# A decoder layer with a state-space mixer: VectorE takes TensorE's share of the state sum in half of the pairs, and the last attention passes use 512-wide exponentials

## The chip, the cores and the metric

The kernel runs on one core of one Trainium2 chip. The metric is the device time of one execution in microseconds (us). A core has TensorE (PE in the profile, with its weight loads as PEld), VectorE (DVE), ScalarE (ACT), GpSimd (POOL) and SyncE (SP), which here issues every DMA. The engines run their own queues in order and meet only at semaphores.

## The reference

All in fp32, on x of shape 4 x 1024 x 512. The line that matters for the change is the sum over 16 states:

```python
u_act = silu(causal_conv(rmsnorm(x) @ in_proj) + b)        # 1024 channels
dt    = softplus(dt_r @ dt_proj.T + b);  A = -exp(A_log)
h_t   = exp(dt_t * A) * h_(t-1) + dt_t * B_t * u_act_t     # per channel, 16 states
y     = sum over n of h[n] * C[n]  +  D * u_act            # the sum
y     = (y * silu(z)) @ out_proj
h     = x + y;  attn = h + (silu(xn@w1) * (xn@w2)) @ w3    # xn = rmsnorm(h)
x     = layernorm(x + attn)
# cross-attention to 64 keys, 16 heads
p     = softmax(QK/sqrt(32));  t = exp(clip(mlp(mean, max, var of p)))   # one t per batch and head
x     = layernorm(x + softmax(QK / (2 t)) V @ Wo)
# a linear layer with top-2 of 8 low-rank experts
x     = layernorm(x + x @ W.T + b + lora(x))
```

The temperature t needs the first softmax over all 1024 positions of a batch.

## The kernel before

**Chunks.** The 4096 positions are cut into 8 chunks (c = 0 to 7) of 512; two chunks make a batch, so t of a batch is known only after both its chunks, and the second attention pass of chunks 6 and 7 can start only when all else is done.

**Streams.** The work is written as six streams of units: `m` (the mixer: convolution, scan, output projection), `l` (the z gate and dt), `y` (SwiGLU MLP, layernorm, queries), `s` (first attention pass: units sc1, mx, e1, sq, ent), and `x` with `w` (second pass: sc2, e2, flip, val, on, fl2, wo, then the expert layer). A planner, `schedule()`, runs at build time: `m_parts()` and `parts()` give each unit's engine, cost in us and predecessors; it merges the streams into one fixed order for each engine, by when a part could start and by a key from `PHASE`, `WORK` and `LOOK`. It also deals out PSUM banks 4 to 7. So every constant in it can move any unit of any stream. `loads()` orders SP's DMAs by the planned times.

**The scan.** Each chunk has 4 pairs of 128-channel blocks, with 16 states each, so 64 steps. A step k of pair p = k // 16 works on a [128, 2, 512] tile of `hb`, a ring of four:

- POOL, `times_b` (L1017): hb = dtu * B, 1024 wide. It waits until the ring's slot, step k - 4, has been summed (`summed`).
- ACT, `decays` (L1081): two 512-wide exponentials to PSUM banks 0 and 1.
- DVE (L1373): two 512-wide scans. Their length differs a little with the chunk's half.
- POOL, `times_c` (L1027): hb = hb * C, 1024 wide.
- the sum, in PSUM banks 2 and 3 (one for each block of the pair). In chunk 0 PE adds both with an identity product (L1679). In chunks 1 to 7 DVE adds the first block (L1389, 512 wide) and PE the second (L1679). PE starts its bank with a product with the diagonal of D (L1675), DVE's bank is started by an ACT copy of u times D (L1161).

After 16 steps `gate` (L1395) reads both banks. An fp32 product is two matmul records in the trace, so the 576 sums and 36 of the diagonal products of the code show up twice each.

**Between two scans** stand the output projection `out` (L1624), `ht` (L1410 and L1057), the turns, the convolution and dt of the next chunk; POOL's part begins again with du (L1042).

**The attention passes.** In the first, for each 128 positions and each half of the heads (8 heads x 64 keys = 512), DVE takes the maxima (L1462), ACT takes 8 exponentials of 64 with their own bias and accumulated sum (L1252), squares all (L1256), and DVE reduces the squares (L1468). In the second, ACT takes 8 exponentials of 64 with the head's scale and bias and an accumulated sum (L1288); then PE turns them (L1739), multiplies with V (L1747), DVE divides (L1512, L1515), PE turns again (L1753), and `wo` (L1577) and `woa` (L1520) follow.

Of the kernel before, what the change touches and what calls it, by code (L numbers as in the profile page):

```python
# [29 lines left out]
FG = 4  # L30
PE, ACT_, DVE, POOL = "PE", "ACT", "DVE", "POOL"
MM, EV, TURN, HOP, FETCH = 0.87, 0.7, 0.95, 0.2, 5.0
# [16 lines left out]
def dve_first(c, k):  # L49

    return c == 0 and k % 2 == 1 and k > 2

# [54 lines left out]
def s_plan():  # L107
    got = []
    for c in range(CHUNKS):
        for t in range(TT):  # L110
            for hf in range(2):
                got += [("sc1", c, t, hf), ("mx", c, t, hf)] + [("e1", c, t, hf, q) for q in range(3)] + [("sq", c, t, hf)]
# [10 lines left out]
def x_plan(chunks):  # L123
    got = []
    for c in chunks:
        def e2(t, hf):
            return [("e2", c, t, hf, 0), ("e2", c, t, hf, 1)]
# [16 lines left out]
def m_parts(u):  # L144
# [13 lines left out]
    elif kind == "turn_in":  # L158
        part(ACT_, 1.6, ("norm", c))
# [4 lines left out]
    elif kind == "conv":  # L164
        if i < JB:
            part(PE, 4 * MM, ("turn_in", c), ("raw", c, i - 4), name=("up", c, i))
# [13 lines left out]
    elif kind == "rms":  # L180
        part(ACT_, 1.6, *(("ht", c, n) for n in c4s))
        part(DVE, 0.2, mine(0))
        part(ACT_, 1.6, mine(1))
    elif kind == "turn_out":
        for n in c4s:
            part(PE, TURN, ("rms", c))
        for n in c4s:
            part(ACT_, EV, mine(n), ("query", c - 1, KC - 1))
# [9 lines left out]
    elif kind == "step":  # L198
# [8 lines left out]
        if i % NS == 0:  # L207
            part(ACT_, 1.1 if c else 0.5, ("gate", c, i // NS - 1), name=("yp", c, i // NS))
# [14 lines left out]
def parts(u):  # L223
# [27 lines left out]
    elif kind == "sp1":  # L251
        part(ACT_, 3.0, ("dt", *key))
    elif kind == "sp2":
        part(DVE, EV, ("sp1", *key))
    elif kind == "sp3":
        part(ACT_, 2.6, ("sp2", *key))
    elif kind == "sp4":
        part(DVE, 1.6, ("sp3", *key), gives=(("dt", *key),) if i > 1 else ())
# [35 lines left out]
    elif kind == "mx":  # L294
        part(DVE, EV, ("sc1", *key))
    elif kind == "e1":
        part(ACT_, 2.4 if u[4] < 2 else EV, ("mx", *u[1:4]), ("ent", c - 1))
    elif kind == "sq":
        part(DVE, EV, ("e1", *key, 2), gives=(("sc1", *key),))
# [11 lines left out]
    elif kind == "temper":  # L311
        part(DVE, 2.3, ("clip", c), ("e2", c - 2, last, 1, 1), gives=(("mlp", c),))
    elif kind == "sc2":
        part(PE, TURN, ("temper", 2 * b + 1), takes=(u,))
    elif kind == "e2":
        part(ACT_, 2.5, ("sc2", *u[1:4]), ("flip", c, i - 1, u[3]) if i else ("lora", c - 1) if c < CHUNKS - 1 else ("flip", c - 1, last, u[3]), ("val", c, i - 2) if i > 1 else ("val", c - 1, TT - 2 + i),
             gives=(("sc2", *u[1:4]),) if u[4] else ())
    elif kind == "flip":
        part(PE, 0.65, ("e2", *key, 1), takes=(u,))
        part(ACT_, EV, mine(), ("val", c, i - 1) if i else ("val", c - 1, last), gives=(u,))  # L320
    elif kind == "val":
        part(PE, 1.7, ("flip", c, i, 0), ("flip", c, i, 1), takes=(u,))
    elif kind == "on":
        part(DVE, 1.0, ("val", *key), ("fl2", c, i - 1) if i else ("fl2", c - 1, last), gives=(("val", *key),))
# [32 lines left out]
PHASE = {'w': (8.408, 8.256, 8.408, 8.256, 8.639, 8.487, 8.639, 8.487), 'y': (6.039, 6.01, 6.125, 6.218, 6.046, 6.01, 6.051, 6.214), 's': (7.437, 6.89, 7.688, 6.881, 7.587, 6.627, 6.484, 6.736), 'x': (8.713, 8.394, 8.925, 8.582, 8.439, 8.453, 9.268, 6.582)}  # L357
# [153 lines left out]
LOOK = {'w': 0.05, 'm': 0.265, 'l': 0.167, 'x': 0, 'y': 0.277, 's': 0.3}  # L511
# [108 lines left out]
def decoder_layer(nc, A, out):  # L620
# [5 lines left out]
    with ctx:  # L626
# [120 lines left out]
        ln_rstd ln_done xl_var xl_sd xl_rstd xl_done sq_ready mx_ready ent_done kb_sum sta_ready tm_pe tm_act tm_dve tempered e2_ready den_ready  # L747
# [21 lines left out]
        def filled(eng, key):  # L769
# [3 lines left out]
            return ps[:, bank]  # L773

# [1095 lines left out]
```

## Time and profile before

| | |
|---|---|
| time, median of 3 runs | 4144.4 us (4144.25 to 4150.9) |
| the profiled execution | 4142.83 us, span 4141.1 us |
| PE busy | 3648.7 us, 88% |
| DVE, ACT, POOL busy | 2527.0 (61%), 2173.9 (52%), 2481.8 (60%) |
| granted TensorE clock, mean | 0.940 |

The span is that of the first to the last instruction. Busy is the union of an engine's instructions. The output projection of chunk c (L1624) starts at 783.18, 1202.09, 1686.54, 2151.99, 2642.29, 3113.04 and 3581.00 us for c = 1 to 7, and near 368 us for chunk 0. From one such start to the next lie the turn to the next chunk and its scan; this stretch is called the period of chunk c + 1. After 3581 us there is no scan left: that is the tail, of 560 us.

### The profile page before, as it was taken

The numbers are of one execution on the slowest core, as the hardware profiler recorded it, in microseconds if no ns is written. First come the engines' busy times: TensorE is split into PE (matmuls) and PEld (weight loads), VectorE is DVE, ScalarE is ACT, GpSimd is POOL, SyncE is SP. The second block draws the span as 40 slices with busy tenths as digits, with TensorE's granted clock in tenths as the row PEclk, the third lists the DMA queues.
The fourth block names the chain that finished last, engine by engine and source line by source line (L and its number), as shares of the span: only waits on it lengthen the run. The fifth ranks groups of instructions, "written<-read, shape, count | busy, mean of one in ns | idle before, by whom it ended". The sixth has DMA issues, their size and how long they took to land.

```text
span 4141.1 us, 35899 instructions
## 1 busy us (share of the span) xinstructions
PE 3648.7 (88%) x9728; PEld 1712.2 (41%) x9728; DVE 2527.0 (61%) x3294; ACT 2173.9 (52%) x5187; POOL 2481.8 (60%) x1101
## 2 busy tenths in 40 slices
PE   7667998799879998999988998999979998999577
PEld 3223443344334445544434335544334434454243
DVE  4784687567746786267765786367774777422222
ACT  5543544664555556565455456574556457431563
POOL 3885599659964995239972996337991997400000
PEclk9889999999999999999989999999989999999788
DMA  5433354335433442234432453234432443212000
GB/s 176 131 123 103 120 165 152 109 116 165 149 111 113 156 156 81 87 105 154 166 117 97 146 162 110 72 115 144 154 125 84 155 153 116 83 58 87 15 1 21
DMA packets 220834, 481.32 MB, mean 116 GB/s; under 512 B 31836, under 2 KB 32220, under 8 KB 220380
## 3 DMA queue, kind: packets, MB, share of 16 engines
q1 hardware_dynamic: 220636, 479.04, 35.1%
q8 instruction: 81, 1.33, 0.1%
q14 instruction: 117, 0.96, 0.1%
HBM read 468.98 MB, written 9.96 MB: 116 GB/s over the span
## 4 chain that ended last, share of the span: by engine, by line
PE 56%; POOL 7%; ACT 7%; DVE 6%; issue 5%; POOLq 0%; DVEq 0%; ACTq 0%
PE ps L1577 31%; PE ps L1664 7%; PE ps L1679 6%; POOL hb L1027 5%; PE ps L1624 5%; DVE hb L1373 2%; POOL hb L1017 2%; PE ps L1712 1%; ACT xw L1288 1%; PE ps L1747 1%; ACT ps L1252 1%; PE ps L1617 1%; PE ps L1793 1%; PE ps L1780 1%; PE ps L1594 1%
## 5 line engine op out<-in xcount | busy, mean ns | idle before, releaser
L1027 POOL TENSOR_TENSOR hb<-hb,bc 128x1024 f32<-128x1024 f32 x512 | 1227.9, 2401 | 127.6 <-issue 86.9
L1017 POOL TENSOR_TENSOR hb<-dtu,bc 128x1024 f32<-128x1024 f32 x481 | 1134.2, 2359 | 192.3 <-PE ps L1679 128.7
L1081 ACT ACTIVATE ps<-dt,a_neg 128x512 f32<-128x512 f32 x1024 | 697.1, 690 | 853.0 <-DVE hb L1373 848.1
L1577 PE MATMUL ps<-fT,wden 128*128 128x512 f32 x2304 | 1042.7, 601 | 16.1 <-DVE hm L1426 6.7
L1679 PE MATMUL ps<-hb,ident 128*128 128x512 f32 x1152 | 656.7, 672 | 249.5 <-POOL hb L1027 248.2
L1577 PEld LDWEIGHTS ps<-fT,wden 128*128 128x128 f32 x2304 | 442.0, 193 | 577.5 <-issue 573.4
L1373 DVE TENSOR_TENSOR_SCAN hb<-ps,state,hb 128x512 f32<-128x512 f32 x512 | 626.5, 1266 | 42.9 <-ACT ps L1081 28.2
L1373 DVE TENSOR_TENSOR_SCAN hb<-ps,hb 128x512 f32<-128x512 f32 x512 | 593.6, 1204 | 12.5 <-POOL hb L1017 9.0
L1389 DVE TENSOR_TENSOR ps<-ps,hb 128x512 f32<-128x512 f32 x448 | 310.9, 694 | 282.7 <-POOL hb L1027 281.8
L1664 PE MATMUL ps<-wden,hm 128*128 128x512 f32 x1024 | 470.5, 606 | 2.1 <-DVE res L1436 1.9
L1577 PE MATMUL ps<-xnT,wmix 128*128 128x512 f32 x1024 | 456.7, 596 | 13.6 <-ACT xnT L1105 8.2
L1679 PEld LDWEIGHTS ps<-hb,ident 128*128 128x128 f32 x1152 | 220.7, 207 | 590.4 <-POOL hb L1027 402.3
L1042 POOL TENSOR_TENSOR dtu<-dt,u 128x1024 f32<-128x1024 f32 x32 | 75.4, 2356 | 536.8 <-issue 466.8
L1664 PEld LDWEIGHTS ps<-wden,hm 128*128 128x128 f32 x1024 | 198.7, 195 | 260.2 <-issue 246.8
L1577 PEld LDWEIGHTS ps<-xnT,wmix 128*128 128x128 f32 x1024 | 193.9, 191 | 253.6 <-issue 253.3
L1624 PE MATMUL ps<-wmix,u 128*128 128x512 f32 x512 | 221.4, 593 | 6.1 <-DVE u L1395 6.1
L1057 POOL TENSOR_TENSOR res<-bc,res 128x512 f32<-128x512 f32 x32 | 39.5, 1269 | 289.6 <-DVE bc L1410 289.6
L1288 ACT ACTIVATE xw<-ps,nm,ftv 128x64 f32<-128x64 f32 x512 | 199.3, 421 | 17.0 <-PE ps L1712 16.7
L1053 POOL TENSOR_TENSOR res<-res,bo_b 128x512 f32<-128x512 f32 x32 | 39.5, 1270 | 241.8 <-PE ps L1691 241.8
L1203 ACT ACTIVATE hm<-ps 128x512 f32<-128x512 f32 x128 | 75.1, 588 | 201.6 <-PE ps L1577 131.1
L1340 DVE SCALAR_TENSOR_TENSOR hb<-hb,cols 128x512 f32<-128x512 f32 x192 | 143.9, 750 | 37.9 <-ACT hb L1124 33.3
L1436 DVE TENSOR_TENSOR res<-ps,res 128x512 f32<-128x512 f32 x128 | 86.4, 678 | 116.2 <-PE ps L1664 115.4
(207 smaller groups left out, 3995.7 us busy)
## 6 DMA issues: line engine op xcount, KB each, us to landing
bc<-bc_dram SPq DMA_DIRECT2D x1024, 256.0 KB, 3.6
wden<-in_w SPq DMA_DIRECT2D x192, 512.0 KB, 3.6
wmix<-in_w_mix SPq DMA_DIRECT2D x96, 512.0 KB, 3.6
watt<-in_w_qof SPq DMA_DIRECT2D x26, 512.0 KB, 4.3
xm<-in_x SPq DMA_DIRECT2D x8, 1024.0 KB, 5.4
res<-in_x SPq DMA_DIRECT2D x8, 1024.0 KB, 6.8
wden<-in_w_qof SPq DMA_DIRECT2D x16, 512.0 KB, 3.5
out<-res SPq DMA_DIRECT2D x8, 1024.0 KB, 4.3
```

Of the source, the lines that this page charges most:

```text
L1017: TTn(hb[:, k % 4], dtu[:, :, :], bc[:, 0, k % 3].unsqueeze(1).broadcast_to([P, 2, CH]), ALU.mult).then_inc(s.s1_ready, 1)
L1027: TTn(hb[:, k % 4], hb[:, k % 4], bc[:, 1, k % 3].unsqueeze(1).broadcast_to([P, 2, CH]), ALU.mult).then_inc(s.s3_done, 1)
L1081: A_(dst, dt[:, p % 2, jj], ACT.Exp, scale=a_neg[:, j, n:n + 1]).then_inc(full_of(key), 1)
L1288: ins = A_(eb[:, hh], bank[:, h], ACT.Exp, bias=nm2[:, TT * half + i, hh:hh + 1], scale=ftv[:, 0, hh:hh + 1], accum_out=den[:, 0, i % 2, h ...
L1340: ins = V.scalar_tensor_tensor(acc[:, j % 3], up[:, j % 2, tap:tap + CH], conv_w[:, j, tap:tap + 1], acc[:, j % 3], ALU.mult, ALU.add)
L1373: V.tensor_tensor_scan(hb[:, i % 4, jj], src, hb[:, i % 4, jj], first, ALU.mult, ALU.add).then_inc(free_of(key), 1)
L1389: V.tensor_tensor(ps[:, 2], ps[:, 2], hb[:, i % 4, 0], ALU.add).then_inc(s.sum_done, 1)
L1436: V.tensor_tensor(res[:, c % 3, tt], src, res[:, c % 3, tt], ALU.add).then_inc(free_of(key), 1)
L1577: ins = M(dst, a, b, start=start and n == 0, stop=stop and n == len(pairs) - 1)
L1624: ins = M(dst[t], u[:, j, t * P:(t + 1) * P], wo, start=j == 0, stop=j == JB - 1)
L1664: ins = M(dst, hm[:, f, tt * P:(tt + 1) * P], wi[:, (f % 2) * 512:(f % 2) * 512 + 512], start=f == 0, stop=f == FG - 1)
L1679: ins = M(dst, ident[:, :], hb[:, i % 4, jj], start=False, stop=n == NS - 1)
```

## The change

1. **The sum.** `dve_sums(c, p)` is true for c > 0 and p in (0, 3). There DVE adds both blocks in one 1024-wide `tensor_tensor` on banks 2 and 3, PE's products for the pair are dropped, and ACT starts both banks with copies of u times D. Those who wait for a sum there (`summed`: POOL, gate) wait for DVE alone. Pairs 1 and 2 and chunk 0 stay.
2. **First pass of chunk 7** (`wide1`): DVE subtracts the maxima from the scores in PSUM (512 wide), ACT takes one exponential of 512 into `hm`, one square, and DVE reduces both (the sums of the exponentials were accumulated by ACT before).
3. **Second pass of chunks 6 and 7** (`wide2`): `temper` also scales the keys by the head's temperature, PE computes the scores after that, DVE shifts them (new unit `sh`, 512 wide), ACT takes one exponential of 512, DVE reduces it (new unit `dn`), and `on` waits for that.
4. **The planner.** Most costs are set anew (a product 0.87 to 0.866, an eviction 0.7 to 0.61, the first pass's exponentials 2.4 to 1.35, the second's 2.5 to 1.54), with some predecessors, `PHASE` and `LOOK`. All orders are planned again.

```diff
-MM, EV, TURN, HOP, FETCH = 0.87, 0.7, 0.95, 0.2, 5.0
+MM, EV, TURN, HOP, FETCH = 0.866, 0.61, 0.96, 0.19, 5.0
+def dve_sums(c, p):
+    return c and p in (0, 3)
+def pe_pairs(c, p):
+    return len([n for n in range(c * PAIRS + p) if not dve_sums(*divmod(n, PAIRS))])
+def wide1(c):
+    return c == CHUNKS - 1
+def wide2(c):
+    return c >= CHUNKS - 2
...
-LOOK = {'w': 0.05, 'm': 0.265, 'l': 0.167, 'x': 0, 'y': 0.277, 's': 0.3}
+LOOK = {'w': 0.08, 'm': 0.247, 'l': 0.167, 'x': 0, 'y': 0.259, 's': 0.355}
...
+            if dve_sums(c, k // NS):
+                return
             if k % NS == NS - 1:
                 filled(eng, ("yp", c, k // NS, 1))
...
-                        A_(dgi[:, p], ident[:, :], ACT.Copy, scale=...).then_inc(s.d_ready, 1)
+                        if dve_sums(c, p):
+                            key = ("yp", c, p, 1)
+                            A_(take(act, key), u[:, 2 * p + 1], ACT.Copy, scale=...).then_inc(full_of(key), 1)
+                        else:
+                            A_(dgi[:, p], ident[:, :], ACT.Copy, scale=...).then_inc(s.d_ready, 1)
...
+                            A_(hm[:, n % FG], ps[:, USE[key][0]], ACT.Exp, scale=DK ** -0.5).then_inc(s.e1_ready, 1)
...
+                        A_(eb[:, 8 * hf:8 * hf + 8], bank, ACT.Exp).then_inc(free_of(key), 1)
...
+                    if both:
+                        V.tensor_tensor(ps[:, 2:4], ps[:, 2:4], hb[:, i % 4], ALU.add).then_inc(s.sum_done, 1)
+                    else:
+                        V.tensor_tensor(ps[:, 2], ps[:, 2], hb[:, i % 4, 0], ALU.add).then_inc(s.sum_done, 1)
...
+                        ins = V.tensor_tensor(src, src, bcast(top, KEYS), ALU.subtract)
...
+                        V.tensor_tensor(keys, keys, bcast(ftv[:, 0], KEYS), ALU.mult)
...
+                elif kind == "sh":
+                    V.tensor_tensor(src, src, bcast(nm2[:, TT * half + i, 8 * hf:8 * hf + 8], KEYS), ALU.add
+                                    ).then_inc(shifted(c), 1)
+                elif kind == "dn":
+                    V.tensor_reduce(den[:, 0, i % 2, 8 * hf:8 * hf + 8], eb[:, 8 * hf:8 * hf + 8], AX, ALU.add
+                                    ).then_inc(s.dn_ready, 1)
...
+                    if dve_sums(c, p):
+                        continue
```

## Rows read from the trace of the kernel before

**Rows 1.** Windows by stage: chunk 0, periods 1 and 2, periods 3 to 7, tail
```profile
core 0: us, PE busy (x) PEld busy (x) DVE busy (x) ACT busy (x) POOL busy (x), PEclk, DMA share, GB/s
...
370.00:1202.00 832.00, 743.82 (x1764) 326.49 (x1762) 567.47 (x681) 430.65 (x878) 626.42 (x276) 0.95 0.41 136
1202.00:3581.00 2379.00, 2191.45 (x5935) 1035.23 (x5936) 1574.79 (x2076) 1332.68 (x3130) 1580.32 (x700) 0.95 0.38 124
3581.00:4141.00 560.00, 456.73 (x1499) 246.12 (x1497) 127.36 (x298) 228.85 (x838) 14.78 (x12) 0.90 0.12 40
```

**Rows 2.** The page's chain that ended last, shares by engine
```profile
PE 56%; POOL 7%; ACT 7%; DVE 6%; issue 5%; POOLq 0%; DVEq 0%; ACTq 0%
```

**Rows 3.** The same windows, only the products with V (L1747) of the second attention pass
```profile
370.00:1202.00 832.00, 0.00 (x0) 0.00 (x0) 0.95 0.41 136
1202.00:3581.00 2379.00, 39.67 (x320) 38.69 (x320) 0.95 0.38 124
3581.00:4141.00 560.00, 23.41 (x192) 22.50 (x192) 0.90 0.12 40
```

**Rows 4.** Groups of instructions by line: busy, mean ns, idle before and its releaser
```profile
L1081 ACT ACTIVATE ps<-dt,a_neg 128x512 f32<-128x512 f32 x1024 | 697.1, 690 | 853.0 <-DVE hb L1373 848.1 <-DVE dt L1361 1.2
L1679 PE MATMUL ps<-hb,ident 128*128 128x512 f32 x1152 | 656.7, 672 | 249.5 <-POOL hb L1027 248.2
L1389 DVE TENSOR_TENSOR ps<-ps,hb 128x512 f32<-128x512 f32 x448 | 310.9, 694 | 282.7 <-POOL hb L1027 281.8
```

**Rows 5.** The chain of the tail, in order of time: start, us, what
```profile
3732.70 27.47 PE ps L1577 x64
...
3902.31 0.61 DVE mxs L1462
...
3940.25 0.70 DVE se L1468
...
3952.97 3.78 ACT xw L1288 x20
```

**Rows 6.** Waits of PE and POOL, first in periods 1 and 2, then 3 to 7: us, times, longest
```profile
PE ps L1679 <- POOL hb L1027: 67.2, 31, 4.3
...
POOL dtu L1042 <- issue: 116.6, 2, 60.6
POOL res L1057 <- DVE bc L1410: 58.7, 2, 29.8
POOL hb L1017 <- PE ps L1679: 19.5, 13, 2.7
...
PE ps L1679 <- POOL hb L1027: 91.7, 47, 4.7
...
POOL hb L1017 <- PE ps L1679: 96.3, 37, 14.5
```

**Rows 7.** Waits of DVE, first in periods 1 and 2, then in 3 to 7
```profile
DVE ps L1389 <- POOL hb L1027: 96.5, 86, 4.1
...
DVE ps L1389 <- POOL hb L1027: 185.3, 192, 4.0
```

**Rows 8.** One line's instructions: durations in ns, min/median/max, first and last start
```profile
L1389 DVE TENSOR_TENSOR ps<-ps,hb x448: 667/699/700, 471.1 to 3564.0; 128x512 f32<-128x512 f32 x150
...
L1380 DVE TENSOR_TENSOR hb<-dtu,bc x31: 1192/1897/3127, 82.7 to 353.2; 128x1024 f32<-128x1024 f32 x31
...
L1027 POOL TENSOR_TENSOR hb<-hb,bc x512: 2332/2356/3406, 82.7 to 3561.6; 128x1024 f32<-128x1024 f32 x171
```

**Rows 9.** Windows of the tail: end of MLP and queries, first pass, second pass
```profile
3884.00:3903.00 19.00, 9.60 (x32) 6.74 (x32) 6.16 (x11) 12.05 (x66) 0.00 (x0) 0.76 0.00 0
3903.00:3945.00 42.00, 0.23 (x1) 0.00 (x0) 13.19 (x26) 26.97 (x144) 0.00 (x0) 0.50 0.00 0
3945.00:4141.00 196.00, 152.35 (x606) 91.97 (x606) 43.10 (x128) 94.49 (x325) 0.00 (x0) 0.86 0.03 11
```

More of the change, by code:

```diff
@@ L111, in s_plan @@
             for hf in range(2):
-                got += [("sc1", c, t, hf), ("mx", c, t, hf)] + [("e1", c, t, hf, q) for q in range(3)] + [("sq", c, t, hf)]
+                got += [("sc1", c, t, hf), ("mx", c, t, hf)] + [("e1", c, t, hf, q) for q in range(2 if wide1(c) else 3)]
+                got.append(("sq", c, t, hf))
         got.append(("ent", c))
@@ L165, in m_parts @@
         if i < JB:
-            part(PE, 4 * MM, ("turn_in", c), ("raw", c, i - 4), name=("up", c, i))
+            old = ("ft", c - 1, i - 2) if c and 2 <= i <= 5 else ("raw", c, i - 4)
+            part(PE, 4 * MM, ("turn_in", c), old, name=("up", c, i))
         if i >= 2:
@@ L207, in m_parts @@
         if i % NS == 0:
[L208 removed]
+            part(ACT_, (1.4 if dve_sums(c, i // NS) else 1.1) if c else 0.5, ("gate", c, i // NS - 1), name=("yp", c, i // NS))
         for jj in range(2):
@@ L255, in parts @@
     elif kind == "sp3":
-        part(ACT_, 2.6, ("sp2", *key))
+        part(ACT_, 2.6 if i > 1 else 1.95 - 0.65 * i, ("sp2", *key))
     elif kind == "sp4":
-        part(DVE, 1.6, ("sp3", *key), gives=(("dt", *key),) if i > 1 else ())
+        part(DVE, 1.42, ("sp3", *key), gives=(("dt", *key),) if i > 1 else ())
     elif kind in ("h", "hv"):
@@ L294, in parts @@
     elif kind == "mx":
-        part(DVE, EV, ("sc1", *key))
+        part(DVE, 2 * EV if wide1(c) else EV, ("sc1", *key))
+    elif kind == "e1" and wide1(c):
+        part(ACT_, EV, ("mx", *u[1:4]), ("sq", c, i - 2, u[3]), ("w3", c, FB // FG - 1, last))
     elif kind == "e1":
-        part(ACT_, 2.4 if u[4] < 2 else EV, ("mx", *u[1:4]), ("ent", c - 1))
+        part(ACT_, 1.35 if u[4] < 2 else EV, ("mx", *u[1:4]), ("ent", c - 1))
     elif kind == "sq":
-        part(DVE, EV, ("e1", *key, 2), gives=(("sc1", *key),))
+        part(DVE, 2 * EV if wide1(c) else EV, ("e1", *key, 1 if wide1(c) else 2), gives=(("sc1", *key),))
     elif kind == "ent":
@@ L773, in filled, with shifted, halves @@
             return ps[:, bank]
+        def shifted(c):
+            return s.sh_last if c == CHUNKS - 1 else s.sh_ready
+        def halves(c, i, hf):
+            return len([n for n in range(c) if wide2(n)]) * 2 * TT + 2 * i + hf
         def emptied(eng, key):
@@ L1384, in _ @@
                     dve.wait_ge(s.s3_done, n + 1)
+                    both = dve_sums(c, i // NS)
                     if i % NS == 0:
                         filled(dve, ("yp", c, i // NS, 0))
+                        if both:
+                            filled(dve, ("yp", c, i // NS, 1))
                     else:
                         dve.wait_ge(s.sum_done, n - STEPS)
-                    V.tensor_tensor(ps[:, 2], ps[:, 2], hb[:, i % 4, 0], ALU.add).then_inc(s.sum_done, 1)
+                    if both:
+                        V.tensor_tensor(ps[:, 2:4], ps[:, 2:4], hb[:, i % 4], ALU.add).then_inc(s.sum_done, 1)
+                    else:
+                        V.tensor_tensor(ps[:, 2], ps[:, 2], hb[:, i % 4, 0], ALU.add).then_inc(s.sum_done, 1)
                 elif kind == "gate":
@@ L1707, in _ @@
                             emptied(pe, ("q", c, c4))
+                    if kind == "sc2" and i == 0 and hf == 0 and wide2(c):
+                        pe.wait_ge(s.tempered, b + 1)
                     T = TT * half + i
```

92 lines of the change are left out of this document (67 added, 25 removed).

## The prediction

> **What bounds the kernel now.** I read the page first, then the chain of waits, then windows cut at the starts of the output projection, then the waits inside them, and last the tail's chain.
>
> No engine is full: PE, the busiest, is busy 88% of the span. The chain that ended last runs 56% of the span on PE and 7% or less on each other engine [rows 2]. The windows show why. A period of chunks 1 and 2 takes 832 / 2 = 416 us with 371.9 us of PE busy; one of chunks 3 to 7 takes 2379 / 5 = 475.8 us with 438.3 us [rows 1]. POOL's work is the same in both, 313 and 316 us. What the later ones have more is the second attention pass and the expert layer, which cannot start before a batch's temperature is known: none of its products with V lie in periods 1 and 2, 320 records (20 tiles) in 3 to 7, the other 12 tiles in the tail [rows 3]. So 66.4 us more of PE work made a period 59.8 us longer: 0.90 us for each us. That is the exchange rate I use for PE work in periods 3 to 7.
>
> In periods 1 and 2 the rate must be lower. POOL is busy 313 us there and waits (116.6 + 58.7) / 2 = 87.7 us between two scans, for the output projection and for the convolution and dt [rows 6]; together 401 us of 416. Those periods hang on POOL's scan and the turn between scans, and PE costs only what POOL visibly waits for it: 19.5 us in both [rows 6].
>
> The tail, 560 us, has no POOL work. PE is busy 456.7 us of it [rows 1], but not evenly: between 3903 and 3945 us PE is busy 0.2 us while the first pass of chunk 7 runs between ACT and DVE, and of the 196 us after that PE is busy 152 [rows 9].
>
> **PE's sums.** The change drops 7 chunks x 2 pairs x (16 identity products + 1 diagonal product) = 238 products. 64 records back to back take 27.47 us, 0.429 each [rows 5], and a product is two: 0.859 us. That is 204 us in all and 34 x 0.859 = 29.2 us a chunk.
> - Periods 3 to 7: 29.2 x 0.90 x 5 = 131 us. Bounds: 73 (half the rate, should the freed time open only where nothing is ready) and 146.
> - Periods 1 and 2: half of the steps lose their wait for PE: half of 19.5 us, 10 us. Bounds 0 and 58 (all of PE's work).
> - PE also stood still for POOL in front of these sums, 91.7 us in periods 3 to 7 [rows 6], since its queue is in order. Half of the sums go, so up to 46 us of it. Some of that waiting would only move to the next thing that isn't ready; I take 20. Bounds 0 and 46.
>
> **DVE's sums.** 224 adds become 1024 wide. The trace has the 512-wide one at 694 ns [rows 4] but not the wide one. Nearest rows: another 1024-wide add or product of DVE took 1192 ns at least and 1897 in the median [rows 8]; two 512-wide adds would be 1388. I take 1.22 us, near the undisturbed 1192, since one start is saved: +0.53 us an add, 8.5 us a pair, 118 us in all. What hides it: DVE waits for POOL in front of its sums 96.5 us in periods 1 and 2, 12.1 us a pair, and 185.3 us in periods 3 to 7, 9.3 us a pair [rows 7]. The mean fits, barely: after it DVE has some 1 to 3 us left in such a pair, and lumps (a row of bn_stats, a wait for `wo`) will now reach the scan that stands behind them in DVE's queue, then POOL's `times_c`, then the ring. I take 20 us. Bounds: 0, and 118 with no cover.
>
> Why not 1897 ns: that instruction (L1380) multiplies two SBUF tensors while POOL runs. The sum reads one operand from PSUM and one from SBUF, and 448 of that kind beside the same POOL work stayed between 667 and 700 ns [rows 8]. The Trainium skill ("SBUF — State Buffer", section "SBUF: two separate sides") says that VectorE and GpSimd share a port pair as an exclusive lock, taken by a VectorE instruction with two SBUF inputs against a GpSimd one that reads SBUF, and not by one with a single SBUF input. By that rule the trace agrees on both: 1192 to 3127 ns for the one kind, a constant 0.7 us for the other. The Trainium skill ("VectorE: DVE Perf Modes", section on the TRN2 errata) gives (N + 151) / 0.96 ns for an fp32 add, 691 ns for 512 (the row has 694) and 1224 ns for 1024; with it the term would stay +0.53 us. If the lock did take the wide sums, see the last rival.
>
> **ACT.** The 14 diagonals become 512-wide copies, some 0.3 us each, 4 us in all; ACT waits 848 us for DVE before its decays [rows 4], which hides it. Uncovered it would be 4 us. No DMA is added or dropped; SP's loads wait for the same releases, now planned at other times.
>
> **The tail.**
> - First pass of chunk 7: 8 half-tiles from 3902.3 to 3941.0 us [rows 5], 38.6 us, 4.83 each, one after the other through ACT and DVE. Wide: DVE has a maximum, a subtraction and two reductions, about 4 x 0.69 = 2.8 us, and ACT 2 x 0.65 = 1.3. In a row with hand-overs that is again 4.8; fully overlapped 2.8 x 8 + 3 = 25. I take -10 (0 to -14).
> - Before it, 3884 to 3903 us, chunk 6's first pass still runs with PE half idle (9.6 of 19 us) [rows 9]. With PE freed earlier it has room to finish sooner: -10 (0 to -19).
> - Second pass of chunks 6 and 7: 196 - 152 = 44 us of PE idle [rows 9]. Ten exponentials of 64 took 3.78 us [rows 5], so a tile's 16 take 6.0; two of 512 take 1.4 (690 ns, [rows 4]) and add 4 x 0.69 on DVE, which is busy only 43 of these 196 us. The layernorms' idle stays. I take -20 (0 to -40).
> - The keys' scaling (1024 wide, 1.2 us) and the scores behind it stand on the only chain there is: +3.
> Together -37; bounds +3 and -73.
>
> **The new order.** All streams are planned again with costs nearer the trace. POOL waits up to 14.5 us for a single PE sum now [rows 6], so orders are far from perfect and could turn out better or worse. I take 0, bounds -40 and +40.
>
> **Sum:** -131 - 10 - 20 + 20 - 37 = -178 us. Profiled execution 4142.8 (span 4141.1 and 1.7 around it): 3964.8. The median of the runs lies 1.6 above it: **3966 us**. A period 3 to 7 would then be near 475.8 - 26 - 4 + 3 = 449 us, still above the 401 us of POOL's work and turn.
>
> **Rivals.**
> 1. *More comes back.* PE's work at its full 146 us, all 46 us of its waits, half of periods 1 and 2's 58 (29), DVE hidden, tail -50: -271, 3873 us. For it: a period has 48 us more of POOL idle to lose. Against: DVE goes from 66% (1574.8 of 2379) to some 74% busy.
> 2. *Half is taken back.* PE's time returns at half the rate (73) and DVE's lumps cost 40, with -10 and -30 elsewhere: -73, 4071 us. For it: long waits of POOL come in pairs where the second pass runs, where DVE itself waits in its queue. Against: the rate of 0.90 is measured on exactly such periods.
> 3. *Nothing.* The critical turn between scans grows by what the scans lose, 0 us: 4144. The sums lie in the scans, where POOL waits 96.3 us for PE [rows 6], so this is unlikely.
> 4. *Slower: the wide add holds POOL.* If each add and POOL's instructions exclude each other, POOL's step grows by 1.22 us, 224 x 1.22 = 273 us, and the other terms (-198 without DVE's 20) leave +75: 4219 us. It decides from 198 / 224 = 0.88 us of POOL time for each add. Against it stand the constant 0.7 us of 448 adds and POOL's median of 2356 beside a minimum of 2332 ns [rows 8].
>
> **Numbers.** Forecast 0.54 (its own range 3915 to 4020), rival 1 0.15, rival 2 0.18, rival 3 0.04, rival 4 and kin 0.09. From rival 1's to rival 2's time, 3880 to 4075, leaves out under 2 in 10. A difference under 0.2% (8 us) could not be told from none here. Faster 0.89, same 0.03, slower 0.08.
>
> **What the profile after would show.** L1679's successor with 1152 - 448 = 704 records, and 448 adds in two forms, 224 at about 1.22 us. POOL's products still at 2.36 us (else rival 4). Output projections some 449 us apart from chunk 2 on, 410 before that. PE's wait for POOL at its sums about halved. The gap of 42 us in PE's work before the temperature cut to 30. It would be wrong if DVE's scans came late: then POOL's `times_c` waits for DVE and PE's idle share grows instead of the period shrinking.

## The result and the profile after

The kernel after takes **4096.67 us** (4081.68 to 4099.33, 4 runs), the kernel before beside it 4147.56 (4144.25 to 4150.9): ratio 0.9876, 95% interval 0.9862 to 0.9891. It is 51 us faster where 178 were forecast, and lies above the range. The profiled execution took 4095.55 us, its span is 4093.8.

The windows of [rows 1], cut at the output projections of the kernel after, and below them those of the products with V alone (x counts records, 16 to a tile):
```profile
core 0: us, PE busy (x) PEld busy (x) DVE busy (x) ACT busy (x) POOL busy (x), PEclk, DMA share, GB/s
366.29:1192.00 825.71, 678.20 (x1632) 303.50 (x1633) 599.32 (x680) 431.74 (x878) 626.34 (x276) 0.92 0.42 137
1192.00:3577.28 2385.28, 2089.87 (x5739) 1005.95 (x5740) 1666.41 (x2079) 1349.14 (x3257) 1580.40 (x700) 0.93 0.38 124
3577.28:4093.80 516.52, 430.70 (x1354) 230.87 (x1353) 155.21 (x344) 137.63 (x333) 14.86 (x12) 0.90 0.12 41
...
1192.00:3577.28 2385.28, 46.21 (x384) 45.77 (x384) 0.93 0.38 124
3577.28:4093.80 516.52, 15.60 (x128) 15.05 (x128) 0.90 0.12 41
```
Against the stages of before (368, 834, 2379, 560 us) chunk 0 is 2 us shorter, periods 1 and 2 are 8 us shorter, **periods 3 to 7 are 6 us longer**, and the tail is 44 us shorter. But 24 tiles of the second pass lie in periods 3 to 7 now, not 20, and 8 in the tail, not 12. PE's work there fell by 102 us and its idle time rose from 188 to 295 us: the freed time stayed empty.

The page's chain by engine, and four of its groups:
```profile
PE 49%; issue 18%; DVE 15%; POOL 10%; ACT 7%; DMA 0%; SPq 0%; POOLq 0%; DVEq 0%; ACTq 0%
...
L1121 ACT ACTIVATE ps<-dt,a_neg 128x512 f32<-128x512 f32 x1024 | 694.6, 691 | 778.0 <-DVE hb L1436 775.9
L1777 PE MATMUL ps<-hb,ident 128*128 128x512 f32 x704 | 388.4, 658 | 122.1 <-POOL hb L1067 122.0
L1456 DVE TENSOR_TENSOR ps<-ps,hb 128x1024 f32<-128x1024 f32 x224 | 274.2, 1224 | 66.6 <-POOL hb L1067 65.9
L1458 DVE TENSOR_TENSOR ps<-ps,hb 128x512 f32<-128x512 f32 x224 | 155.4, 694 | 137.6 <-POOL hb L1067 137.0
```
PE's share of the chain fell from 56 to 49% and "issue", time without a visible wait, rose from 5 to 18% [rows 2]. 704 records and a wide add of 1224 ns are as forecast.

POOL's waits in periods 3 to 7 of before (two rows that the prediction read only for periods 1 and 2), then of after, then PE's waits there of after:
```profile
POOL dtu L1042 <- issue: 350.2, 5, 92.8
POOL res L1057 <- DVE bc L1410: 181.0, 5, 42.7
```
```profile
POOL dtu L1082 <- issue: 354.4, 5, 87.9
POOL res L1097 <- DVE bc L1481: 217.3, 5, 52.8
POOL hb L1067 <- issue: 55.5, 27, 8.0
POOL hb L1057 <- PE ps L1777: 54.1, 23, 16.7
POOL hb L1057 <- DMA bc<-bc_dram: 50.4, 13, 17.7
POOL hb L1057 <- DVE ps L1456: 26.1, 6, 10.0
...
PE ps L1673 <- DVE se L1547: 56.7, 2, 30.6
PE ps L1760 <- DVE res L1507: 47.3, 14, 8.0
PE ps L1789 <- ACT res L1266: 16.5, 2, 8.3
PE ps L1777 <- POOL hb L1067: 11.5, 15, 1.7
```
The first two rows of POOL are the turn between two scans; it grew from 531 to 572 us. POOL's waits inside the scans, for PE's sums and others, are the rest. PE's stall for POOL in front of its sums fell from 91.7 [rows 6] to 11.5 us, and PE stands in front of other heads of its queue instead: twice up to 30.6 us for the reduction of a first attention pass (`se`).

The chain of the tail at the end of the first pass of chunk 7, and PE's waits in the tails of before and after:
```profile
3881.75 0.61 DVE mxs L1534
...
3885.66 0.61 DVE mxs L1534
...
3889.57 0.61 DVE mxs L1534
```
```profile
PE ps L1722 <- DVE sta L1491: 42.1, 1, 42.1
```
```profile
PE ps L1822 <- DVE sta L1570: 30.3, 1, 30.3
```
A half-tile (128 positions, half of the heads) takes 3.9 us, not 4.83.

### The profile page after: what moved, and what is told of

Read it like the earlier page. It is cut to its first block, busy times and chain, and to the rows that moved or that the text cites. A ratio compares the mean times of both kernels' runs of the same rounds, so it can differ in the third digit from the quotient of the medians.

```text
span 4093.8 us, 34623 instructions
## 1 busy us (share of the span) xinstructions
PE 3452.0 (84%) x9252; PEld 1643.2 (40%) x9252; DVE 2681.9 (66%) x3343; ACT 2100.1 (51%) x4810; POOL 2481.4 (61%) x1101
## 4 chain that ended last, share of the span: by engine, by line
PE 49%; issue 18%; DVE 15%; POOL 10%; ACT 7%; DMA 0%; SPq 0%; POOLq 0%; DVEq 0%; ACTq 0%
PE ps L1673 26%; DVE hb L1436 8%; PE ps L1760 8%; POOL hb L1067 6%; PE ps L1720 6%; PE ps L1777 4%; POOL hb L1057 3%; DVE ps L1456 1%; PE ps L1812 1%; ACT xw L1351 1%; DVE hb L1443 1%; ACT ps L1121 1%; PE ps L1893 1%; PE ps L1880 1%; PE ps L1847 1%
## 5 line engine op out<-in xcount | busy, mean ns | idle before, releaser
L1067 POOL TENSOR_TENSOR hb<-hb,bc 128x1024 f32<-128x1024 f32 x512 | 1228.2, 2401 | 106.7 <-issue 55.5
L1057 POOL TENSOR_TENSOR hb<-dtu,bc 128x1024 f32<-128x1024 f32 x481 | 1132.9, 2357 | 177.5 <-PE ps L1777 72.2
L1673 PE MATMUL ps<-fT,wden 128*128 128x512 f32 x2304 | 1031.1, 600 | 27.8 <-DVE res L1507 7.0
L1760 PE MATMUL ps<-wden,hm 128*128 128x512 f32 x1024 | 492.6, 630 | 86.6 <-DVE res L1507 62.8
L1673 PE MATMUL ps<-xnT,wmix 128*128 128x512 f32 x1024 | 470.3, 610 | 87.0 <-DVE se L1547 56.7
L1777 PE MATMUL ps<-hb,ident 128*128 128x512 f32 x704 | 388.4, 658 | 122.1 <-POOL hb L1067 122.0
L1456 DVE TENSOR_TENSOR ps<-ps,hb 128x1024 f32<-128x1024 f32 x224 | 274.2, 1224 | 66.6 <-POOL hb L1067 65.9
L1777 PEld LDWEIGHTS ps<-hb,ident 128*128 128x128 f32 x704 | 135.3, 205 | 326.8 <-POOL hb L1067 194.2
L1458 DVE TENSOR_TENSOR ps<-ps,hb 128x512 f32<-128x512 f32 x224 | 155.4, 694 | 137.6 <-POOL hb L1067 137.0
L1720 PE MATMUL ps<-wmix,u 128*128 128x512 f32 x512 | 230.6, 612 | 9.6 <-DVE u L1464 9.6
L1812 PE MATMUL ps<-kbd,qT 128*128 128x256 f32 x512 | 142.3, 417 | 90.4 <-DVE se L1547 72.4
L1093 POOL TENSOR_TENSOR res<-res,bo_b 128x512 f32<-128x512 f32 x32 | 39.6, 1269 | 216.2 <-PE ps L1789 216.2
```

What stands on the lines that cost most here:

```text
L1057: TTn(hb[:, k % 4], dtu[:, :, :], bc[:, 0, k % 3].unsqueeze(1).broadcast_to([P, 2, CH]), ALU.mult).then_inc(s.s1_ready, 1)
L1067: TTn(hb[:, k % 4], hb[:, k % 4], bc[:, 1, k % 3].unsqueeze(1).broadcast_to([P, 2, CH]), ALU.mult).then_inc(s.s3_done, 1)
L1456: V.tensor_tensor(ps[:, 2:4], ps[:, 2:4], hb[:, i % 4], ALU.add).then_inc(s.sum_done, 1)
L1458: V.tensor_tensor(ps[:, 2], ps[:, 2], hb[:, i % 4, 0], ALU.add).then_inc(s.sum_done, 1)
L1673: ins = M(dst, a, b, start=start and n == 0, stop=stop and n == len(pairs) - 1)
L1720: ins = M(dst[t], u[:, j, t * P:(t + 1) * P], wo, start=j == 0, stop=j == JB - 1)
```

## The experiments

All times are medians; behind each stands its ratio to the kernel before, measured beside it, with the 95% interval. POOL's time in periods 3 to 7 is set out for most of them at the end of this section. "Orders of before" means that planner, costs, start times and look-aheads are those of the kernel before.

### 1. The move alone, in the orders of before

```diff
+def dve_sums(c, p):
+    return c and p in (0, 3)
...
+                        V.tensor_tensor(ps[:, 2:4], ps[:, 2:4], hb[:, i % 4], ALU.add).then_inc(s.sum_done, 1)
```


> The kernel before with every engine's order as it was, only the sums moved: in pairs 0 and 3 of chunks 1 to 7 VectorE adds both blocks, TensorE none. Theory A (the time lies in the fixed orders: freed TensorE time opens where nothing is ready behind the head of its queue, and only a new order can use it): 4110 to 4150 us. Theory B (TensorE's time does come back, VectorE's longer adds take it away again): also near 4150, but then e2 is far below. Theory C (my forecast: 0.9 us for each us of TensorE): 4147 - 141 = about 4005 us.

Measured: 4125.0 us, 0.9954 (0.9939 to 0.9969). 204 us of PE's work moved, 20 us back.

The same, but VectorE's add stays 512 wide (`ps[:, 2]`, `hb[:, i % 4, 0]`), so that nothing is added to it:

> As e1, but VectorE's add stays 512 wide, so the second block's state terms are left out in those pairs: TensorE's relief without VectorE's cost. Theory A: within 25 us of e1. Theory B: 80 us or more below e1 (118 us of VectorE time is gone). Theory C: 20 us below e1.

Measured: 4104.5 us, 0.9902 (0.9886 to 0.9919), 41 us. So the relief of PE by itself comes back at 41 / 204 = **0.20** in this order, and VectorE's 118 us cost 20. Both times lie where theory A had them, and far from theory C, the forecast's.

### 2. The change's order without parts of the change

The sums back on PE once the orders are made:
```diff
 MIXER, BEGUN, DONE, ORDER, DENSE_TAKES = schedule()
+def dve_sums(c, p):
+    return False
```


> The kernel after with its orders and its wide exponentials as they are, but the sums made as before (TensorE adds the second block everywhere). Theory A: the new order carries most of the gain, so little is lost by putting 204 us of TensorE work back: 4100 to 4150 us. Theory C: 4097 + 131 + 10 + 20 - 20 = about 4240 us. Theory B: TensorE's 204 us come back and VectorE's 118 go: 4150 to 4200 us.

Measured: 4146.4 us, 1.0004 (0.9994 to 1.0014). The new order, the new costs and the wide exponentials together are worth nothing, and the move is worth 49 us *in this order*, against 20 in the other. POOL's waits in periods 3 to 7 of this run:
```profile
POOL dtu L1087 <- issue: 351.4, 5, 86.7
POOL res L1102 <- DVE bc L1486: 223.1, 5, 58.6
POOL hb L1062 <- PE ps L1782: 178.6, 51, 18.5
POOL hb L1072 <- issue: 50.6, 21, 8.0
```
The change's order makes POOL wait 178.6 us for PE's sums (before: 96.3 [rows 6]); the move takes 124 of them away, and 50.4 us for the DMA of the B rows (4.3 in this run) and 26.1 us for VectorE's wide sums stand there then. Net, these periods are 40 us shorter.

VectorE's add cut to 512 in the change's order (as in 1):

> The kernel after with VectorE's wide adds cut to 512, the second block's state terms left out in those pairs: 118 us less VectorE work in the same order. Theory A: 4097 less 10 to 30 us. Theory B: 4097 less 80 us or more. Theory C: 4097 less 20.

Measured: 4071.3 us, 0.982 (0.9803 to 0.9837): the widening costs 25 us. From 4146.4 to 4071.3 the relief of PE alone is worth 75 us in this order, 75 / 204 = **0.37**, against 0.20 in that of before: the rate belongs to the order as much as to the engine.

The exponentials left as they were, the orders planned without them:
```diff
 def wide1(c):
-    return c == CHUNKS - 1
+    return False
 def wide2(c):
-    return c >= CHUNKS - 2
+    return False
```


> The kernel after without any 512-wide exponential (both passes as before in chunks 6 and 7; the planner then moves only units of the tail). Forecast's term: the wide passes are worth 37 us, so 4097 + 37 = 4134 us. Rival: the tail is shorter because four tiles of the second pass were planned out of it, and the wide passes are worth 5 to 15 us: 4102 to 4112 us.

Measured: 4102.4 us, 0.9901 (0.988 to 0.9922). The intervals overlap with that of after; in the profiles the tail is 529.8 us in place of 516.5, with 8 tiles in both. The wide exponentials are worth some 6 to 13 us.

### 3. What a microsecond of each engine is worth, in the orders of before

The output product of the second attention pass, one of four products (the others' terms are missing):
```diff
-group(dst, [... for c4 in range(KC)])
+group(dst, [... for c4 in range(1)])
```


> The kernel before, same orders, with the attention's output projection cut from four products to one a tile (three quarters of that sum left out): 3 x 0.859 us x 32 tiles = 82 us less TensorE work, 52 of it in periods 3 to 7, but on the chain of the second pass, which VectorE waits for at the head of its queue. Theory A (what counts is the round trip of a tile, not TensorE's total): 0.6 us or more for each us there, so 4145 - 31 - 20 in the tail or better, 4095 or less. Rival (TensorE time returns at 0.2 wherever it is saved, as in the relief at the sums): 4145 - 10 - 20 = 4115 us.

Measured: 4096.8 us, 0.9887 (0.9871 to 0.9904).

The MLP's hidden layers, three of four products:
```diff
-group(dst, [... for ci in range(KC)]
+group(dst, [... for ci in range(KC - 1)]
```


> The kernel before, same orders, with one of the four products left out of each first-layer sum of the MLP (a quarter of these sums left out): 32 x 0.859 = 27.5 us less TensorE work a chunk, about as much as the change takes, but in another stream. Theory A (bulk TensorE time returns at about 0.2 in the scans, and fully in the tail, where TensorE is busy without a break): 4145 - 27 - 0.2 x 192 = 4080 us. Forecast's rate of 0.9 in periods 3 to 7: 4145 - 27 - 124 - 11 = 3983 us.

Measured: 4071.4 us, 0.9828 (0.9814 to 0.9843).

ScalarE, the second pass's 16 exponentials a tile as 4 of 256 columns:
```diff
-for h in range(4 * q, 4 * q + 4): A_(eb[:, hh], bank[:, h], ACT.Exp, bias=..., scale=..., accum_out=...)
+A_(eb[:, hh:hh + 4], bank[:, h:h + 4], ACT.Exp, scale=0.01, accum_out=...)
```


> The kernel before, its orders unchanged; in the second attention pass of every chunk the 16 exponentials of 64 columns per row tile (one for each head: 421 ns and 221 ns for the sum) become 4 of 256 columns, with a constant scale of 0.01 and no bias in place of the head's own scale and bias; the denominators of the other 12 heads are a constant 1.0. It takes some 5 to 7 us of ScalarE's work off each of the 32 row tiles: about 200 us in all, two fifths of it in the tail (388 of 1033 instructions). Theory A (ScalarE's exponentials set the tail's pace, as I put it in the prediction for the wide passes): 12 tiles in the tail save 4 us each or more, the tail falls by 48 us or more, and periods 1 to 7 give less than 20. Theory B (the tail's pace is the round trip of the tiles through all the engines, of which the exponentials are a part that overlaps the other half's): the tail falls by 10 to 30 us. Theory C (the instruction order fixed beforehand leaves every relief unused): under 10 us in all, 4135 to 4147 us.

Measured: 4118.7 us, 0.9943 (0.9929 to 0.9958). ACT's busy time fell by 150 us, not 200 (the row of the sum, 221 ns, overlaps the exponential), the tail by 14.

GpSimd:
```diff
-TTn(hb[:, k % 4], hb[:, k % 4], bc[:, 1, k % 3]...broadcast_to([P, 2, CH]), ALU.mult)
+TTn(hb[:, k % 4, :, 0:448], hb[:, k % 4, :, 0:448], bc[:, 1, k % 3, 0:448]...broadcast_to([P, 2, 448]), ALU.mult)
```


> The kernel before, its orders unchanged; GpSimd's scaling of the states (512 times, 128x1024, 2401 ns) works on 448 of each 512 columns, so that an eighth of the products with the C rows is left out: about 0.29 us less each time, 2.3 us per pair's four steps two by two, some 130 us in periods 1 to 7 and 150 us in all. Nothing of PE, VectorE or ScalarE changes. Theory A (GpSimd, busy 65% of these periods, sets the pace of the 16 steps, and waits only for the turn between chunks): 0.7 or more of the 130 us comes back, and 0 to 20 us in the first chunk, 4025 to 4055 us. Theory B (no engine does: each step waits for a chain through ScalarE, VectorE, GpSimd and PE whose order is fixed beforehand): about what TensorE's relief gave, 0.2 to 0.4, which is 4090 to 4120 us. Theory C (GpSimd has slack enough): 4135 us or more.

Measured: 4101.2 us, 0.9907 (0.9887 to 0.9928). One group of this run's page:
```profile
L1028 POOL TENSOR_TENSOR hb<-hb,bc 128x896 f32<-128x896 f32 x512 | 1086.8, 2125 | 164.2 <-issue 107.2
```
and its windows of chunk 0, periods 1 and 2, and 3 to 7:
```profile
0.00:355.30 355.30, 251.28 (x529) 101.37 (x529) 259.04 (x240) 181.32 (x342) 242.02 (x113) 0.90 0.45 146
355.30:1176.20 820.90, 745.55 (x1768) 327.40 (x1769) 566.18 (x681) 430.07 (x878) 592.50 (x276) 0.95 0.43 137
1176.20:3536.10 2359.90, 2180.44 (x5934) 1035.82 (x5935) 1566.05 (x2076) 1331.69 (x3130) 1495.45 (x700) 0.96 0.39 125
```
Chunk 0 gives 12.7 us for 64 x 0.276 = 17.7 us of relief, a rate of 0.72, so that there the pace is mostly GpSimd's. Periods 3 to 7 give 19 for 88. GpSimd doesn't set their pace either.

| run | engine, us of work | time, us | rate |
|---|---|---|---|
| sums | PE 204 (476 records) | 41 | 0.20 |
| output product | PE 82 (192 records) | 46 | 0.56 |
| hidden layers | PE 220 (512 records) | 71 | 0.32 |
| scaling | POOL 137 | 38 | 0.28 |
| exponentials | ACT 150 | 24 | 0.16 |
| VectorE's widening (added) | DVE 118 | 20 to 25 | 0.17 to 0.21 |

PE's work is counted as records times 0.429 us [rows 5]; its busy time fell by 196, 63 and 169 us. The mean granted clock was 0.924, 0.933 and 0.933 in these runs, 0.940 before, so that the records that are left took longer. Of POOL and ACT it is the fall in busy time, of DVE 224 x 0.53.

A rate in this table is a mean over stages. In the profile of the hidden layers' run, PE is busy 109 us less in periods 3 to 7 and they are 39 us shorter (0.36); in the tail it is busy 31 us less and the tail is 31 us shorter. So in the tail this work of PE comes back whole, as that run's expectation had it, and the 0.32 is no rate of the periods.

Then reliefs together. The sums and the scaling:

> The orders of before, with two reliefs at once: the second block's state terms left out in pairs 0 and 3 of chunks 1 to 7 (TensorE 204 us less; alone -41 us), and GpSimd's scaling of 448 of 512 columns (some 141 us less; alone -40 us). The second block's terms and an eighth of the products with the C rows are missing. Theory 1 (the engines take turns as the bound): more than the sum, -110 us or more, 4030 us or below. Theory 2 (chains of latencies in a fixed order, reliefs add up): -70 to -95 us, 4048 to 4073 us. Less than the sum, -60 or less (4083 us or more), would say that both shorten the same waits, in front of something that neither touches.

Measured: 4048.5 us, 0.9763 (0.9744 to 0.9783), 98 us by the ratio against 41 + 38. That is 19 us more than the sum, and the three intervals together leave some 14 open: in part these two do cover for each other, though the time still lies at the edge of what theory 2 had.

And with the hidden layers and the exponentials on top:

> The orders of before, with four reliefs at once: the second block's terms left out in pairs 0 and 3 of chunks 1 to 7 (alone -41 us), GpSimd's scaling of 448 of 512 columns (-40), three of four products in the MLP's hidden layers (-71), and exponentials of half a bank with a constant scale in the second attention pass (-22). The sum of the single ones is -174 us. Theory 1 (turns as the bound): -230 us or more, 3910 us or below. Theory 2 (chains of latencies, reliefs add up): -150 to -195 us, 3948 to 3993 us. Less than -130 us: the reliefs meet in the same waits, in front of something that none of them touches (VectorE's chain, a transfer, the order).

Measured: 3960.0 us, 0.9551 (0.9532 to 0.9569), 186 us against 174 for the four alone. The four add up, within what their intervals leave open. So it is not one engine, and engines that cover for each other are at most a small part: the account that fits is many waits, each shortened a little by the relief that touches it.

### 4. What the order is worth

The sums not moved, but start times and look-aheads searched anew (by the planner's own total) with the change's costs:
```diff
 def dve_sums(c, p):
-    return c and p in (0, 3)
+    return False
-PHASE = {...}; LOOK = {...}
+PHASE = {...}; LOOK = {'w': 0.228, 'm': 0.252, 'l': 0.092, 'x': 0.13, 'y': 0.258, 's': 0.419}
```


> The kernel after with the sums made as before the change (TensorE adds the second block everywhere), the new costs and the wide passes, and LOOK and PHASE chosen anew for that case. If the sums' move is worth what the forecast said, some 140 us, it cannot come near: 4220 us or more. If its worth is the 30 to 50 us that old and new order each showed, and the rest is a question of the order chosen: 4120 to 4145 us.

Measured: 4100.9 us, 0.9896 (0.9881 to 0.991), below both ranges: the gain of the change without the move.

The change with `PHASE` and `LOOK` of before:

> The kernel after with the two lines of start times and look-aheads of before, so that the order follows from the planner with its new costs but not from a new search; its planned total is 4203 us, that of the change 4079 us. If the moved sums make the gain, whatever the order: 4095 to 4110 us. If the search makes it, and the planner's total is a guide to 20 us or so: 4160 to 4220 us, slower than the kernel before.

Measured: 4189.7 us, 1.0104 (1.0087 to 1.0121). All of the change but its search is 45 us *slower* than before; ten tiles are left for the tail (566.6 us), and in one place POOL waits 85.6 us for PE's turns before it adds the bias `bo_b` (L1093), with the next scan's work behind that in its queue.

A search that may also choose the pairs, in two results, one with 12 and one with 10 of 28 pairs:
```diff
-    return c and p in (0, 3)
+    return (c, p) in ((1, 0), (2, 0), (2, 1), (2, 2), (3, 0), (4, 0), (4, 2), (6, 0), (7, 0), (7, 3))
```


> The kernel after, with another choice of the pairs of which VectorE adds both terms, (1,0), (2,0) to (2,3), (3,0), (4,0), (5,0), (6,1), (6,2), (7,0) and (7,3) as (chunk, pair), 12 of 28 in place of 14, and with look-aheads and start times found anew for that choice; the planner's own total for it is 4060 us, 19 us under its total for the kernel after (4079 planned, 4094 measured). If the order of the work is what decides, as the run without the moved sums but with its own order showed (4100.9 us), a further 10 to 30 us come off: 4065 to 4090 us. If the planner's total is no guide within 20 us (it had 4109 for that run), 4085 to 4115 us.

Measured: 4066.7 us, 0.9819 (0.9802 to 0.9836).

> As the run before it, with VectorE's wide additions in 10 of 28 pairs, (1,0), (2,0) to (2,2), (3,0), (4,0), (4,2), (6,0), (7,0) and (7,3), and look-aheads and start times of its own; the planner's total is 4061 us. By the same reasons 4065 to 4090 us if the order decides and the planner's total follows it, 4085 to 4115 us if the planner is no guide to within 20 us. If the number of moved pairs itself decided, it would lie above the kernel after by some 4/14 of 50 us, about 4110 us.

Measured: **4048.4 us, 0.9774 (0.9754 to 0.9793)**, faster than both kernels and below all that was expected, with fewer pairs moved. Periods 1 and 2, 3 to 7, and the tail:
```profile
369.10:1193.40 824.30, 697.77 (x1632) 308.01 (x1633) 598.71 (x681) 431.77 (x878) 626.28 (x276) 0.92 0.43 137
1193.40:3524.20 2330.80, 2102.99 (x5850) 1001.60 (x5851) 1618.07 (x2074) 1355.17 (x3261) 1580.13 (x700) 0.96 0.39 126
3524.20:4054.50 530.30, 445.89 (x1379) 239.34 (x1377) 158.47 (x349) 138.47 (x333) 14.83 (x12) 0.89 0.13 42
```
The same order with the sums back on PE (edit as in 2):

> The kernel of the run with 10 moved pairs (4048.4 us), every order of it kept, but all sums back on TensorE and VectorE's additions all 512 wide: TensorE gets 10 x 14.6 = 146 us more, VectorE 84 us less. If the order alone made the 92 us and the move is worth nothing, as the run without moved sums but with its own order seemed to say: 4048 to 4060 us. If the move is worth in this order what it was worth in the change's own (49 us for 14 pairs, 3.5 us a pair): 4075 to 4090 us. If TensorE is the bound of this better order, 0.6 of 146 us or more: 4135 us or more.

Measured: 4107.8 us, 0.9914 (0.9898 to 0.9931), between the last two ranges. The 10 pairs are worth 59 us in this order, 5.9 us each; the 14 of the change 49 in its own, 3.5 each; 20 in that of before, 1.5 each.

### 5. Which pairs

In the order with 10 pairs, pair 3 stays on PE in chunks 1 to 6. Pair 3 is the last before the output projection, for which everything waits. PE's windows over the 60 us before the projections of chunks 1 and 2, of before and then of after:
```profile
723.00:783.00 60.00, 40.62 (x100) 0.83 0.38 132
1142.00:1202.00 60.00, 41.01 (x98) 0.83 0.41 132
```
```profile
716.00:776.00 60.00, 24.11 (x60) 12.37 (x60) 49.84 (x47) 34.97 (x99) 55.50 (x25) 0.70 0.40 132
1132.00:1192.00 60.00, 24.05 (x56) 12.18 (x57) 45.49 (x45) 34.88 (x108) 52.23 (x23) 0.67 0.37 126
```
(busy time of PE is the first number behind the length, PEclk the first without a bracket behind the busy times), and the projections of chunks 1 to 3 in the chain of after:
```profile
776.63 29.61 PE ps L1720 x64
1192.00 30.14 PE ps L1720 x64
1647.55 27.47 PE ps L1720 x64
```
Before, all seven took 27.47 to 27.72 us. Two runs ask whether pair 3 is a bad choice. Pairs 0 and 1 in place of 0 and 3, orders of before, otherwise the first run of 1:

> The kernel with the moved sums in the orders of before, but with pairs 0 and 1 moved in place of 0 and 3 (that one: 4125 us, ratio 0.9954). Theory P (the clock at the output projection is a real part of what is lost): the projections of chunks 1, 2 and 4 fall from 29.3 to 30.2 back to 27.7 us, 6 us together, and the time lies 6 us or more below: 4119 us or less. Theory Q (the place of the pair does not matter): 4120 to 4130 us. If pair 1 lies more under the streams that fill TensorE than pair 3, more comes off, up to 20 us.

Measured: 4099.2 us, 0.9892 (0.9875 to 0.9908): 45 us for as many moved sums, where pairs 0 and 3 gave 20. All projections are back at 27.5 to 27.8 us; that makes 6 of the 25 us. POOL's turns are 8 us shorter in periods 3 to 7, 4 of the same 6 among them. The rest is spread (periods 2 and 5 some 10 us each) and wasn't taken apart.

The change's order, pair 0 alone:

> The kernel after with every order kept, but only pair 0 of chunks 1 to 7 added by VectorE; pair 3's sums stay on TensorE. With both on TensorE it took 4146.4 us, with both moved 4096.7: 49 us. Theory P (pair 3 in front of the output projection gives less than its share, since the clock falls): pair 0 alone gives more than half, 4105 to 4117 us. Theory Q (both alike): 4118 to 4126 us. Above 4130 us: most of the gain is pair 3's, whose sums stand in front of the output projection in TensorE's queue.

Measured: 4104.7 us, 0.99 (0.9883 to 0.9918): pair 0 alone gives 42 of the 49 us, pair 3 the other 8. The intervals of this run and of the kernel after overlap, so that the 8 could be near nothing; that it is far less than pair 0's share is clear. In the profiles four projections are slow with both pairs moved and one (29.4 us) with pair 0 alone, 8 us together.

### POOL's time in periods 3 to 7

Length = POOL busy + the turn's waits (for du and for `ht`) + the rest, its waits inside the scans; the last column is the part of the rest that ends with a sum of PE.

| run | length | busy | turn | rest | for PE's sums |
|---|---|---|---|---|---|
| before | 2379 | 1580 | 531 | 267 | 96 |
| moved, orders of before | 2362 | 1580 | 539 | 243 | 12 |
| same, VectorE's add 512 wide | 2348 | 1579 | 537 | 232 | 15 |
| pairs 0 and 1, orders of before | 2347 | 1579 | 530 | 238 | 49 |
| hidden layers, three products | 2340 | 1579 | 526 | 235 | 71 |
| output product, one of four | 2360 | 1580 | 521 | 258 | 99 |
| GpSimd's scaling 448 wide | 2360 | 1496 | 531 | 333 | 122 |
| four reliefs | 2273 | 1493 | 527 | 253 | 22 |
| change's order, sums on PE | 2425 | 1581 | 575 | 269 | 179 |
| change's order, pair 0 | 2395 | 1580 | 573 | 242 | 99 |
| after | 2385 | 1580 | 572 | 233 | 54 |
| order without the move | 2339 | 1580 | 553 | 207 | 97 |
| best order, sums on PE | 2367 | 1581 | 586 | 201 | 121 |
| best order, 10 pairs | 2331 | 1580 | 583 | 168 | 74 |

No relief shortens the turn by more than 10 us (the output product's), most by 5 or less; reliefs live mainly in the rest. What replaces PE there is seen with VectorE's add 512 wide in the orders of before, in POOL's waits of its periods 3 to 7:
```profile
POOL hb L1029 <- DVE ps L1409: 32.1, 5, 14.8
POOL hb L1029 <- DMA bc<-bc_dram: 26.3, 15, 11.7
POOL hb L1039 <- DVE hb L1389: 20.1, 3, 9.5
POOL hb L1039 <- ACT state L1169: 19.4, 13, 3.5
```
PE's 96 us are down to 15. VectorE's sum takes 32 us, where before no wait of `times_b` ended with it, VectorE's scan 20 where it had 3, the loads 26 where they had 16.

## Why the prediction was wrong

The direction was right, the size was not, and the 4096.7 us lie nearest to rival 2 (half is taken back, 4071), though not by its terms. Of the 127 us that were missed, some 92 are the move's (-131 - 10 - 20 + 20 = -141 forecast, -49 in the change's order), and some 37 are the tail's with the order's (-37 forecast, nothing measured for both together).

- **The step that failed is the exchange rate**: "0.90 us for each us. That is the exchange rate I use for PE work in periods 3 to 7", and with it the term of 131 us. Measured, the relief of PE comes back at 0.20 for these sums in the old order and at 0.37 in the change's, and at 0.32 and 0.56 for other products. In periods 3 to 7 it gave 31 us in the old order and 65 in the change's; with VectorE's widening 17 and 40. The comparison that gave 0.90 was between periods with and without the second attention pass. Those differ by more than PE's work. POOL's account has the difference: of the 59.8 us, 18.5 are a longer turn (106.2 in place of 87.7 us), 38.4 are longer waits inside the scans (53.5 in place of 15.1), 3 POOL's own. Of these waits PE's sums ended 19.3 a period, and 9.8 in periods 1 and 2 [rows 6], so that 9.5 of the 59.8 us name the sums; the others ended with VectorE, ScalarE, loads or nothing that the profile names. So the new streams lengthened the periods through all engines, and taking away one engine's work doesn't give that back.
- **The right rule stood beside it.** For periods 1 and 2 I let PE cost "only what POOL visibly waits for it", half of it for half the steps: forecast -10, measured -8 (-12 for the relief alone in the old order). By that rule periods 3 to 7 would have got 48 us (half of 96.3), at most 96. Measured: 31 without VectorE's widening. The 131 us stood above all that POOL waited for these sums. (The term's lower bound of 73 us is half of the full 146; half the rate would be 66.)
- **PE's stalls, -20**: the stall in front of the sums fell by 80 us, far more than the 46 allowed, yet PE's idle time in these periods grew by 107 us: the standing moved to the heads of other units. Here, time that PE idles in its queue wasn't time on the path.
- **VectorE's sums, +20**: 20 us in the old order, 25 in the new; 1224 ns an add, forecast 1.22. Right. The estimate of 1224 ns by the formula of the Trainium skill ("VectorE: DVE Perf Modes", section on the TRN2 errata) is what the row now shows.
- **Rival 4 (the add holds POOL)**: GpSimd's two groups kept means of 2401 and 2357 ns beside 224 wide adds. False, as the row of 448 narrow ones said, and as the rule of the Trainium skill on the shared port pair ("SBUF — State Buffer", section "SBUF: two separate sides") would have it.
- **The tail, -37**: it lost 44, but for another reason: four tiles moved out of it into period 7. With 8 tiles in both, the wide exponentials made 13 us of the tail. First pass: -7 (forecast -10). PE's gap before the temperature: 30.3 us (forecast 30). The second pass's -20 and the +3 behind it came to some -6 together: the exponentials overlap the other half's work, as their run in 3 shows, 14 us of the tail for 56 us of ScalarE's work there.
- **The new order, 0, bounds 40 either way**: within its bounds for the change's order with the sums on PE (0 us with the wide exponentials; in the profiles +46 in periods 3 to 7 and -45 in the tail), but no term of a sum. The move is worth 20, 49 or 59 us by the order, the change with the start times and look-aheads of before is 45 us slower than the kernel before, and an order without the move, with the wide exponentials, makes as much as the whole change. The bounds were too narrow and the order was the larger question.
- **A cost that I didn't see**: pair 3 stands in front of the output projection. The clock there, and whatever else hangs on that pair, leave it 8 of the 49 us, and moving pair 1 in its place gains 25 us in the old order.
- **What the profile was to show**: POOL's products and the 704 records came as forecast. The projections stand 477 us apart and not 449. The sign of being wrong came by half: PE's idle time grew, but POOL's `times_c` waited only 16.1 us for VectorE's scans (2.8 before), so late scans weren't the main cause.

What stays open: why the turn is 40 to 55 us longer in both new orders (periods 4 and 6 hold one tile more each, 3 and 5 one less and period 7 four more, but no run separates the tiles from the rest of the order); the 19 us of pair 3 that the clock doesn't explain; and how good an order without the move could be, since only one was searched for.

## What to carry to other kernels

The price of an engine's work isn't the difference between two stages that differ by whole streams. Write one account along the engine that carries the recurrence (here GpSimd: its work, the turn, its waits by releaser), and allow a relief at most the waits that name it, then ask which releaser is next behind each: here about a third of them came back in periods 3 to 7, less with VectorE's cost. Where a planner orders in-order queues, measure the edit in the old order and the order without the edit before believing either, and try which instances to move: in the same order, pair 1 in place of the pair in front of the product for which all wait was better. That fewer pairs were faster too isn't shown apart from their order, which was searched anew.

## What the hardware showed unexpectedly

Work taken off PE just ahead of a critical product makes that product slower. With PE busy 24.1 of the 60 us ahead of it in place of 40.6, the granted clock of that stretch was 0.70 in place of 0.83, and the 64 records that followed took 29.61 us in place of 27.72: they began at the lower of the two levels, 1.2 GHz (granted 0.50), and were at 2.4 GHz some 4 us later, as PE's windows over the start of that projection show:
```profile
776.63:780.00 3.37, 3.37 (x4) 0.50 0.00 0
780.00:783.00 3.00, 3.00 (x8) 0.93 0.00 0
783.00:786.00 3.00, 3.00 (x9) 1.00 0.00 0
```
It costs 2 to 3 us in four of eight projections. With pairs 0 and 1 moved, or in the order with 10 pairs, all projections took 27.5 to 27.8 us; with the change's order and the sums on PE one of them still took 29.41. So it is the clock at the start of the product that counts, and the mean over the 60 us ahead doesn't settle it: in the run with the move in the orders of before, the projection of chunk 6 followed 60 us with a granted clock of 0.66 and still took 27.6 us, PE having run without a break in the last of them. And GpSimd's 1024-wide product stayed at 2357 ns whatever VectorE added beside it.
